# Two-pass graph network: score scatters issued in the first pass's gather loop, score scans put ahead of the node adds

## The reference

```python
h = jnp.einsum('ni,hio->nho', x, W_att)
e = jnp.einsum('eho,ho->eh', h[src], a_src) + jnp.einsum('eho,ho->eh', h[dst], a_dst)
e = jax.nn.leaky_relu(e, NEG_SLOPE)
alpha = _segment_softmax(e, dst, N)                 # max, exp, sum per destination
out = jax.ops.segment_sum(alpha[:, :, None] * h[src], dst, num_segments=N).mean(axis=1)
...
for _ in range(num_hops):                           # two hops of averaging
    h = jax.ops.segment_sum(h[src], dst, num_segments=N) / deg
```

## Time and profile before

| what | value |
|---|---|
| median of 3 runs | 5745.7 us (5740.72 to 5746.71) |
| span of the profiled execution | 8265.0 us |
| busy in the span: PE, DVE, ACT, POOL | 5626.1, 4830.5, 3994.5, 4210.8 us |
| first pass ends (last row store issued) | 1212.34 us |
| second pass's first gather | 1296.44 us |
| mean granted TensorE clock | 0.797 |

### The profile page before, as it was taken

The page is one execution under the profiler, slowest core; times in us unless marked ns, Lnnn a source line. Parts: engine busy times, 40 slices in busy tenths (PEclk is TensorE's granted clock), DMA queues, the critical chain, the costliest instruction groups (busy, mean ns, idle before and its releaser), DMA issues.

```text
span 8265.0 us, 131597 instructions
## 1 busy us (share of the span) xinstructions
PE 5626.1 (68%) x48815; PEld 4887.9 (59%) x48820; DVE 4830.5 (58%) x12173; ACT 3994.5 (48%) x6886; POOL 4210.8 (51%) x4251
## 2 busy tenths in 40 slices
PE   6777772333333777776778867787767777677886
PEld 5666652222222677765777766776756777567775
DVE  5555565665665555655656665555645565556665
ACT  3444443655554355553555544555535555355553
POOL 4444447666664455553555545554445455445554
PEclk8888885555556788886899878888968888788887
DMA  3323324766765223322233322232213223232332
GB/s 83 81 76 84 85 79 146 256 228 234 239 236 190 55 77 80 81 78 54 78 80 81 79 64 75 77 80 76 81 50 79 78 77 80 54 79 77 81 81 62
DMA packets 508836, 828.41 MB, mean 100 GB/s; under 512 B 112922, under 2 KB 219424, under 8 KB 495142
## 3 DMA queue, kind: packets, MB, share of 16 engines
q1 hardware_dynamic: 372854, 650.98, 23.3%
q0 software_dynamic: 135344, 169.01, 11.2%
HBM read 385.16 MB, written 434.48 MB: 99 GB/s over the span
## 4 chain that ended last, share of the span: by engine, by line
PE 45%; issue 20%; DVE 16%; another core or an unknown queue 11%; ACT 4%; DMA 2%; POOL 1%; SPq 1%; ACTq 0%; DVEq 0%; POOLq 0%
PE psum L1347 28%; PE psum L1157 8%; DVE arena L1750 6%; PE psum L1361 4%; DVE by_lane L1812 2%; ACT arena L898 2%; PE psum L1132 1%; DVE arena L1685 1%; DVE arena L1480 1%; DVE psum L1795 1%; PE psum L1142 1%; POOL agg L693 1%; DMA by_lane<-attr_last 1%; ACT arena L832 1%
## 5 line engine op out<-in xcount | busy, mean ns | idle before, releaser
L686 POOL DMA_INDIRECT gring<-tableh,src_i x2652 | 2613.9, 986 | 2669.1 <-DVE psum L1795 1687.1
L1347 PE MATMUL psum<-penalty,arena 125*128 125x192 bf16 x24736 | 2672.0, 259 | 725.2 <-issue 696.4
L1347 PEld LDWEIGHTS psum<-penalty,arena 125*128 125x128 bf16 x24736 | 2223.4, 103 | 983.8 <-issue 921.2
L686 POOL DMA_INDIRECT gring<-table,src_i x1364 | 1376.8, 1009 | 1092.9 <-issue 410.7
L1750 DVE TENSOR_SCALAR arena<-dst_f,node_id 125x640 bf16<-125x640 f16 x4556 | 1600.9, 400 | 0.1
L1789 DVE TENSOR_REDUCE gring<-psum 128x128 f32<-128x384 f32 x505 | 356.0, 705 | 2104.3 <-remote 1112.9
L960 ACT COPY psum<-diag 128x512 f32<-128x512 f32 x505 | 297.5, 590 | 2492.0 <-DVE psum L1795 2383.1
L1361 PE MATMUL psum<-arena 128*128 128x128 f32 x4040 | 702.3, 314 | 197.7 <-issue 148.6
L1361 PEld LDWEIGHTS psum<-arena 128*128 128x128 f32 x4040 | 605.0, 222 | 264.0 <-issue 261.9
L1480 DVE SCALAR_TENSOR_TENSOR arena<-psum,be_c,arena 128x512 f32<-128x512 f32 x505 | 376.6, 746 | 450.5 <-ACT arena L832 279.2
L1812 DVE TENSOR_TENSOR_SCAN by_lane<-mask_x,psum 128x256 f32<-128x256 f32 x1010 | 632.7, 667 | 0.2
(11 more groups left out here) (271 smaller groups left out, 7682.8 us busy)
## 6 DMA issues: line engine op xcount, KB each, us to landing
rows<-arena SPq DMA_DIRECT2D x101, 1296.0 KB
acts<-arena SPq DMA_DIRECT2D x505, 256.0 KB
arena<-acts SPq DMA_DIRECT2D x505, 256.0 KB
rowsg<-run SPq DMA_DIRECT2D x505, 256.0 KB
gring<-tableh,src_i POOLq DMA_INDIRECT x2652
dst_f<-pe_src SPq DMA_DIRECT2D x430, 93.8 KB
rows<-run SPq DMA_DIRECT2D x101, 256.0 KB
gring<-table,src_i POOLq DMA_INDIRECT x1364
```

Of the source, the lines that this page charges most:

```text
L686: pool.indirect_dma_start(ring[:, s, k, :], None, table, bass.IndirectOffsetOnAxis(ap=src_i[:, c * K + k:c * K + k + 1], axis=0))\
L1347: ins = mm(found(n)[:, m, :], hot_at(n // 2, j)[:, at:at + P], parts[:, j, :, :].rearrange("q a f -> q (a f)"), start=(j == 0), stop=(j == ...
```

## The change

The 25 scatters of destination scores leave the stretch between the passes. A function `scatter_scores` is called once per chunk in POOL's loop of the first pass, behind the chunk's gathers: in chunks 58 to 82 it issues one scatter each, in chunk 83 the gather of the rows' first scores. In chunk 58 it first waits for the slots, for the stores of the scores and for the zeros in `ed_edges`. On SP the load of `sm_a` is put ahead of the five stores of table 2. On DVE the copy of `ed0` and the four scans are put ahead of the five node adds.

```diff
+SCATTER = 2 * NJ + 8
@@ sync
             load_nat(CH + 1)
+            sp.wait_ge(ed_scattered, NJ * 16)
+            sp.wait_ge(cross_sb, NJ)
+            sp.dma_start(sm_a, ed_edges[0:EP, :].rearrange("(p t) h -> p t h", p=P)).then_inc(edx_in, 16)
             for g in range(NG):
                 sp.wait_ge(t2_ready, g + 1)
 ...
-            sp.wait_ge(ed_scattered, NJ * 16)
-            sp.wait_ge(cross_sb, NJ)
-            sp.dma_start(sm_a, ed_edges[0:EP, :].rearrange("(p t) h -> p t h", p=P)).then_inc(edx_in, 16)
@@ gpsimd
+            def scatter_scores(j):
+
+                if j == 0:
+                    pool.wait_ge(last_ready, 1)
+                    pool.wait_ge(slots_ready, 1)
+                    pool.wait_ge(ed_out, 16)
+                    pool.wait_ge(ed_zeroed, 96)
+                    settle()
+                if 0 <= j < NJ:
+                    pool.indirect_dma_start(ed_edges, bass.IndirectOffsetOnAxis(ap=slot_i[:, j:j + 1], axis=0),
+                                            ed_all[:, j, :], None).then_inc(ed_scattered, 16)
+                if j == NJ:
+                    pool.indirect_dma_start(ed0[:, :], None, ed_nodes,
+                                            bass.IndirectOffsetOnAxis(ap=dst_i[:, 0:1], axis=0)).then_inc(ed0_in, 16)
 ...
                 gather_chunk(c, c % SL, table1, gather1, g1_ready, K - k1(c))
+                scatter_scores(c - SCATTER)
             for s in range(SL):
                 pool.wait_ge(rows1_out[s], 16 * uses(s))
-            pool.wait_ge(last_ready, 1)
-            pool.wait_ge(ed_zeroed, 96)
             settle()
             gather_nodes(rows1, agg_all, agg_in)
-
-            pool.wait_ge(slots_ready, 1)
-            pool.wait_ge(ed_out, 16)
-            settle()
-            for j in range(NJ):
-                pool.indirect_dma_start(ed_edges, bass.IndirectOffsetOnAxis(ap=slot_i[:, j:j + 1], axis=0),
-                                        ed_all[:, j, :], None).then_inc(ed_scattered, 16)
-            pool.indirect_dma_start(ed0[:, :], None, ed_nodes,
-                                    bass.IndirectOffsetOnAxis(ap=dst_i[:, 0:1], axis=0)).then_inc(ed0_in, 16)
@@ vector
+            dve.wait_ge(edx_in, 16)
+            dve.wait_ge(ed0_in, 16)
+            st.then(nc.vector.tensor_copy(sm_a[:, 0, :], ed0[:, :]))
+            for h in range(H):
+                st.done(nc.vector.tensor_tensor_scan(sm_b[:, :, h], mask[:, :], sm_a[:, :, h], 0.0, ALU.mult, ALU.add))
+
             for g in range(NG):
                 dve.wait_ge(agg_in[g], GJ * 16)
 ...
-            dve.wait_ge(edx_in, 16)
-            dve.wait_ge(ed0_in, 16)
-
-            st.then(nc.vector.tensor_copy(sm_a[:, 0, :], ed0[:, :]))
-            for h in range(H):
-                st.done(nc.vector.tensor_tensor_scan(sm_b[:, :, h], mask[:, :], sm_a[:, :, h], 0.0, ALU.mult, ALU.add))
```

## The result

The changed kernel takes 5757.04 us (median of 17 runs) against 5745.7 us: ratio 1.0015, 95% interval 1.0008 to 1.0022. That is 8.6 us slower by the ratio (0.0015 x 5745.7; 3 to 13 us by its interval, 11.3 us by the medians), where 5737.5 us was forecast. It is rival B's result (+7.5 us, 5753 us). Three of the 17 runs took 6201, 6740 and 8678 us at a granted clock of 0.65 to 0.78 instead of 0.88, and the ratio is that of the other 14.

What follows compares the result with a forecast made beforehand. Plain runs were taken to go at bare-work pace, PE and POOL nearly level in the first pass, POOL pacing the second. -25.8 us gained plus 17.6 paid in the loop gave -8.2: 5737.5 us, range 5708 to 5757.

Steps and rivals of the forecast that it cites:

- rival B: First pass: POOL already paces it, so all 33.3 us are paid and 25.8 come back; +7.5, 5753 us; chance 0.20.
- The long execution and its gaps: Whole profile: 2562 us of "issue" and unknown queue hardly occur in plain runs, leaving 5703 us at bare-work pace.
- POOL paces the second pass: Second pass: its gathers fill nearly all of a plain run, so the gain is POOL's 25.8 us, not 38.5.
- The score path: Between the passes: sweeps start earlier, so the exponential comes 39.5 us and the first messages 38.5 us earlier.
- What the first pass pays: First pass, chunks 58 to 83: 26 added POOL instructions, partly hidden, cost the loop 17.6 us of 33.3.
- The lead of 10 us: First pass: POOL's gathers run ahead through the ring, cushioning 10 of the 27.6 us it falls behind.
- What POOL gains at its start: Between the passes: POOL starts the second pass near 1274.6 instead of 1296.44, 21.8 us earlier.
- the 2.9 us from store to POOL: Between the passes: delay from table 2's last store to POOL's start, taken from the first pass's last row store.
- What POOL no longer loses beside DVE: Start of second pass: gathers lose 9.1 us beside DVE's sweeps instead of 13.1, saving 4.0 us.
- A: Rival, first pass: the loop hides the scatters; gain 25.8 to 38.5 us, time near 5711 us; chance 0.32.
- C: Rival, first pass: each scatter is held to 1.28 + 0.45 us in the loop; +19, 5765 us; chance 0.12.
- What would show it: Signs in the changed profile: single scatters at 0.97 us, 11 us POOL idle, no 34 us DVE wait, span 26 to 38 us shorter.

Runs made afterwards that it cites:

- before, again: The unchanged kernel, profiled once more on a chip where it takes about 5745 us; 5759.23 us in its profiled execution, median there 5744.05 us.
- e5: Kernel before plus two unrelated memsets on POOL behind the gathers of each of chunks 58 to 83; 5772.51 us, ratio 1.0044.
- e10: Changed kernel with each store of table 2 cut into 112 and 13 partitions; 5750.66 us, ratio 1.0011 to the kernel before.
- e11: Kernel before with 8 scatters and the ed0 gather in the loop, 4 before the row-store wait, 13 behind the node gathers; 5745.89 us, ratio 0.999.
- e12: Changed kernel with table 2's stores cut in two and its last four scatters moved from the loop to before POOL's row-store wait; 5753.59 us, ratio 1.0004.
- e1: The kernel before, unchanged, run again for a trace; 8276.69 us, beside a median of 8269.23 us on that chip.
- e2: Changed kernel without the 25 scatters and SP's wait for them; 8252.17 us, ratio 0.9982 to the kernel before.
- e4: Kernel before with the scatters in POOL's loop, the sm_a load and the scans in their old places; 8288.32 us, ratio 1.0027.

## Why the prediction was wrong, step by step

**The long execution and its gaps: right in direction, the figure partly luck.** The unknown queue is gone from the chain, "issue" has shrunk, and in both passes a plain run is paced by POOL's bare work. The account of 8265 - 2562 = 5703 us came within 0.7% of the median, but not by the working that it gave: the page of before, again still has 6% "issue", some 345 us, and PE's busy time, which the prediction left as it was, is 4737.6 us there instead of 5626.1, at a granted clock of 0.883 instead of 0.797.

**POOL paces the second pass: right.** The score path gained 39.8 us (forecast 39.5), the first messages wait for gathers, and without the scatters the kernel gained 27 to 30 us (forecast 25.8), not 39.8.

**What the first pass pays: the step that failed.** The sum took 17.6 us; measured are 34.5. Of its inputs, the scatter's cost was nearly right (1.28 forecast; 1.30 on POOL and 1.33 to 1.35 in the loop's length measured). Wrong was "POOL falls behind by 26 x (8.16 - 7.1) = 27.6 us; less a lead of 10". The chunk time of 7.1 us was a good value (298.0/42 = 7.10), but it was POOL's own pace, not one to which POOL had slack. The 6.88 us came from the median gather, 5.5 x 1.25; of the 143 gathers of chunks 58 to 83 in the kernel before, again, 17 take 1.03 to 1.25 us and 7 take 1.33 to 1.36, which with the others makes the mean chunk 5.5 x 1.29. The lead of 10 us cannot exist on an engine that paces the loop: POOL never waits there before the change, and the 26.7 us that e5's 26.5 us of work add to the loop show that there was none. The prediction had this as rival B and gave it 0.20 against "the lead built up over the first 58 chunks". A step earlier already gave PE 6.6 to POOL's 6.88; the larger was POOL's, and a lead is built only by an engine that is faster than its consumer.

**What POOL gains at its start: too high by 10.4 us.** 21.8 us forecast, 11.4 measured. DVE's part was right: the last node add ended 59.0 us after the last row store, forecast 1271.5 - 1212.3 = 59.2. What failed was the 2.9 us from store to POOL, taken from one store of 256 KB. Five stores of 315 KB each behind one another let POOL go 13.6 us after the issue of the last began. Before, POOL's 26 instructions covered this; the change took the cover away, and the prediction costed it at a small store's price.

**What POOL no longer loses beside DVE: too low by 11.9 us.** 4.0 forecast, 15.9 measured. Of these, 11.5 us come in the first 17 gathers, those beside DVE's scans and sweeps, and are the same error's other side: since POOL starts later, it has one sweep beside it where the forecast had four. e10 shows the exchange: 8.5 us earlier, 6.1 us more lost. The other 4.4 us are spread over the next 83 gathers, whose median is the same; the forecast had nothing for them, and their cause is open. So the errors nearly cancel, 25.8 against 27.3 us: that this part came out right is luck.

**Sum.** -8.2 forecast; + 16.9 for the loop, + 10.4 for the landing, - 11.9 for the sweeps gives the +7.2 us of the account.

**The rivals.** B: 33.3 - 25.8 = +7.5, measured 34.5 - 27.3. A, that the loop hides the scatters, fell with e5. C, that a scatter is held in the loop, needed 1.43 us each; their median duration is 996 ns beside 972 behind the node gathers, and each cost 1.33 to 1.35 us. The range ended at 5757.0 us, where the median lies; by the ratio the time is 5754.3 us.

**What would show it.** The scatters stand singly in the loop at 1.0 us, the load of `sm_a` comes right behind the cross copies and DVE's 34 us are gone, as said. POOL's idle time behind the node gathers is 20.9 us, not 11. The span's fall of 26 to 38 us could not be seen: the trace of the changed kernel is of the other kind of execution.

## What to carry to other kernels

Before a cost is put down to an engine's slack, see that the profile is of the same kind of execution as the time to be explained: 448 us of waits on POOL were none in an execution of the right length. Where a sum over bare durations puts two engines within 5% of each other, as here, reckon with the case that the fuller one has no slack and that every instruction added there is paid whole. Look for a real wait first: four instructions put into one (e11, e12) seem to have cost nothing, where those in the loop cost 1.33 us each. When work is taken out from behind a chain of stores, it stops hiding their landing: time the last of the chain, not one like it.

## What the runs showed of the hardware that was not expected

- The same kernel takes about 5745 us on the chips of e5 to e12 and about 8270 us on that of e1, e2 and e4, with and without a profile; in the long kind the chain has 13 to 20% "issue", the granted clock is 0.80 instead of 0.88, and POOL's waits for DVE and ACT in the first pass are 400 us or more instead of none. The cause is open; no run was made to find it.
- POOL's indirect DMAs go at one per DVE instruction beside float32 operations of 3200 elements with two inputs (3.1 to 3.7 us for 0.94), and at 1.43 us beside the masked scans. The Trainium skill, "SBUF — State Buffer", "Who interferes with whom", has the contention of a two-input DVE instruction with GpSimd's reads; the trace agrees, and shows its size. Of 8.5 us by which POOL started earlier under such sweeps in e10, 6.1 were lost again.
- A memset on POOL behind an indirect DMA starts within its 0.30 us gap, so two of them, 1.22 us together, cost 1.02.
- Five stores of 125 partitions had landed 17.3 us after the first was issued, with a third of the 16 DMA engines busy (0.33); cut into 112 and 13 partitions, 8.9 us (0.83).
